# Attention and feed-forward block on 8 cores: the softmax normalisation of a group of heads moved behind the next group's first exponentials

## The reference

```python
qkv = encodings @ attn_w.T + attn_b
q, k, v = split(qkv per head)                      # heads of 64
scores = einsum('bhki,bhqi->bhkq', k, q) / sqrt(64)
scores = where(key <= query, scores, -10000.0)
probs = softmax(scores, over keys)
combined = einsum('bhkq,bhkl->bhql', probs, v)
x = x + combined @ out_w.T + out_b
...
s = layernorm(x) @ Win + bin_                      # 1024 -> 64
h = relu(s[..., None] * W1 + b1)                   # 64 x 16
g = einsum('btmh,mh->btm', h, W2) + b2
x = x + g @ Wout + bout
```

## Time and profile before

| what | value |
|---|---|
| three runs, median (lowest to highest) | 4349.49 us (4315.81 to 4365.05) |
| the profiled execution | 4315.81 us |
| its span on the slowest core (core 1) | 4313.9 us |
| spans of the 8 cores | 4290.3 to 4313.9 us |
| busy: TensorE, its weight loads, VectorE, ScalarE, GpSimd | 65%, 25%, 26%, 42%, 4% |
| mean granted clock of TensorE (1.0 is 2.4 GHz) | 0.760 |

### The profile page before, as it was taken

The page is one execution under the profiler, slowest core; times in us unless marked ns, Lnnn a source line. Parts: engine busy times, 40 slices in busy tenths (PEclk is TensorE's granted clock), DMA queues, the critical chain, the costliest instruction groups (busy, mean ns, idle before and its releaser), DMA issues.

```text
span 4313.9 us, 40195 instructions; the slowest of 8 cores (4290.3 to 4313.9 us)
## 1 busy us (share of the span) xinstructions
PE 2800.6 (65%) x12288; PEld 1074.8 (25%) x12288; DVE 1110.9 (26%) x2486; ACT 1804.1 (42%) x2945; POOL 167.3 (4%) x324
## 2 busy tenths in 40 slices
PE   0657576586656658677674766767667576765874
PEld 0223232232222223222231322223222132322321
DVE  3141321401324141230223223132132413214112
ACT  0324337166141624617523261643733234272481
POOL 0000000000000000000000000000000000000000
PEclk9768688698676868778776776878877677776886
DMA  6010000100101010010000001000000100000000
GB/s 198 11 38 19 23 30 15 42 7 15 40 20 40 15 35 15 16 40 10 20 30 30 30 20 40 10 20 30 15 25 25 35 25 25 30 15 30 10 10 25
DMA packets 38984, 122.02 MB, mean 28 GB/s; under 512 B 9658, under 2 KB 9786, under 8 KB 38780
## 3 DMA queue, kind: packets, MB, share of 16 engines
q0 software_dynamic: 21504, 67.13, 4.4%
q1 hardware_dynamic: 17020, 51.80, 4.1%
q10 hardware_dynamic: 256, 0.52, 0.0%
HBM read 85.34 MB, written 34.08 MB: 28 GB/s over the span
## 4 chain that ended last, share of the span: by engine, by line
PE 48%; ACT 15%; DVE 12%; issue 11%; DMA 11%; DVEq 0%; ACTq 0%; SPq 0%; POOLq 0%; POOL 0%
PE P L314 10%; PE P L389 10%; ACT s_probs L361 7%; DMA s_zz<-zscr 7%; PE P L291 6%; PE P L448 6%; PE P L352 5%; DVE s_xln L219 2%; DMA zscr<-s_zz 2%; ACT s_zz L407 2%; ACT s_zz L404 2%; DVE s_comb L425 2%; DVE s_probs L491 2%; PE P L543 2%; PE P L547 2%
## 5 line engine op out<-in xcount | busy, mean ns | idle before, releaser
L361 ACT ACTIVATE s_probs<-P 128x1024 bf16<-128x1024 f32 (+3 forms) x1280 | 1063.5, 895 | 376.9 <-PE P L356 305.7
L389 PE MATMUL P<-s_probs,s_vaug 128*65 128x512 bf16 (+3 forms) x2560 | 720.7, 399 | 173.4 <-DVE s_comb L425 94.8
L352 PE MATMUL P<-s_q,s_k 64*128 64x512 bf16 (+3 forms) x1280 | 464.8, 391 | 435.6 <-ACT s_probs L361 402.1
L369 DVE TENSOR_TENSOR s_probs<-s_probs,s_tril 128x256 bf16<-128x256 bf16 x512 | 145.8, 292 | 1403.8 <-ACT s_probs L361 1400.9
L448 PE MATMUL P<-s_ow,s_comb 128*128 128x512 bf16 x1024 | 357.9, 509 | 190.1 <-DVE s_comb L425 150.9
L356 PE MATMUL P<-s_q,s_k 64*128 64x512 bf16 (+3 forms) x1280 | 473.9, 398 | 0.0
L314 PE MATMUL P<-s_xlnT,s_wqk 128*128 128x512 bf16 x2048 | 448.8, 381 | 0.0
L389 PEld LDWEIGHTS P<-s_probs,s_vaug 128*65 128x65 bf16 x2560 | 247.9, 119 | 536.8 <-issue 441.1
L237 ACT ACTIVATE s_stats<-s_stats 128x1 f32<-128x1 f32 x128 | 37.7, 295 | 762.6 <-DVE s_stats L234 762.6
L480 PE MATMUL P<-s_id,s_xln 128*128 128x128 bf16 x512 | 107.9, 258 | 370.9 <-ACT s_probs L487 279.1
L425 DVE TENSOR_TENSOR s_comb<-P,s_zz 64x512 bf16<-64x512 f32 x256 | 174.9, 683 | 643.8 <-DMA s_zz<-zscr 639.5
(11 more groups left out here) (58 smaller groups left out, 2024.9 us busy)
## 6 DMA issues: line engine op xcount, KB each, us to landing
s_x<-x SPq DMA_DIRECT2D x64, 512.0 KB, 3.7
s_zz<-zscr POOLq DMA_DIRECT2D x256, 128.0 KB, 3.0
out<-s_x POOLq DMA_DIRECT2D x64, 512.0 KB, 2.9
s_x<-wqk_t SPq DMA_DIRECT2D x16, 512.0 KB, 7.6
s_x<-wv_t SPq DMA_DIRECT2D x8, 512.0 KB, 6.2
s_x<-ow_t SPq DMA_DIRECT2D x8, 512.0 KB, 7.2
zscr<-s_zz ACTq DMA_DIRECT2D x128, 4.0 KB
s_x<-bias_rows SPq DMA_DIRECT2D x1, 260.0 KB
```

The source lines that it names most:

```text
L352: s.op("pe", lambda E, c=hp, k=kt, c0=col0, S=SC: E.matmul(S[:, c0:512], s_k[0:64, c * T + k * 128: c * T + (k + 1) * 128], s_q[0:64, c * ...
L361: texp = s.op("act", lambda E, S=SC, pb=prb, c0=col0: E.activation(pb[:, :].rearrange("p (h c) -> p h c", h=2, c=512)[:, :, c0:512], S.rea ...
L369: dep_pv = s.op("dve", lambda E, pb=prb, c0=col0: E.tensor_tensor(pb[:, :].rearrange("p (h c) -> p h c", h=2, c=512)[:, :, c0:c0 + 128], p ...
L389: P=pv_banks[bank]: E.matmul(P[:, c0:512], s_vaug[:, ti * NH * 65 + hh2 * 65: ti * NH * 65 + hh2 * 65 + 65], pb[:, hi2 * 512 + c0: hi2 * 5 ...
```

## The change

The normalisation of a group is put into a function `norms`, whose arguments hold the group's pairs and its last value products, and is not called at the end of the group. It is called in the next group's loop, once the scores and exponentials of key tile 0 of both pairs have been issued and before those of key tile 1. For the last group of a stage it is called after the loop over u, where it stood before.

```diff
@@ attention
             comb_written = []
+            pending_norms = None
             for u in range(4):
...
                         newpend = (kt, col0, deps_pv, probs)
+                        if kt == 0 and pending_norms is not None:
+                            pending_norms()
+                            pending_norms = None
                     if pending is not None:
...
                     pending = newpend
-                for pi, hp in enumerate(pairs):
+
+                def norms(pairs=pairs, t_last_pv=t_last_pv):
+                  for pi, hp in enumerate(pairs):
                     t_lp = t_last_pv[pi]
...
                     st_["zz_read"][pi] = comb_written[-1]
+
+                pending_norms = norms
+            pending_norms()
             st_["P1_freed"] = comb_written[-1]
```

## The result

| | before | after |
|---|---|---|
| median of 12 runs each | 4341.80 us | 4408.16 us |
| ratio after to before (95% interval) | | 1.0204 (1.0163 to 1.0245) |
| the profiled execution | 4315.81 us | 4408.10 us |
| span of its slowest core | 4313.9 us | 4406.2 us |
| mean granted clock of that core | 0.760 | 0.756 |

The changed kernel is 2% slower. Between the two profiled executions lie 92.3 us.

What follows compares the result with a forecast made beforehand. No engine bounds the span; each group step ends with the chain Ln, Exp, write, broadcast, multiplication. 36 x 2.4 + 12 x 0.8 = 96 us gave 4412 on the profiled execution's scale, 4445 on the median's; range 4400 to 4505.

Steps and rivals of the forecast that it cites:

- The count and the place: Cost only at 48 steps between head groups: 36 long, 12 short (stages of 4 key tiles); stage ends unchanged.
- Ln 2.4 us later: On ScalarE at each group step, Ln starts behind two exponentials of key tile 0: 1021.65 instead of 1019.24.
- The chain behind Ln is only shifted: Write, broadcast and multiplication keep their distances after Ln, so each long step grows by 2.4 us.
- Short step +0.8: In 4-key-tile stages, masks of key tile 0 ahead of the multiplications get back 1.6 of 2.4 us.
- Sum 96 us, 4412 on the profiled execution's scale: All steps: 36 x 2.4 + 12 x 0.8 us, added to the profiled execution's 4315.8 us.
- The figure on the median's scale: The 96 us sum added to 4349.5 us, the median of three earlier runs: 4445 us.
- The clock is neutral: TensorE's granted clock in the group steps was taken to add or save nothing.
- clock rival: TensorE's clock returns later (4507 us; 0.14, shared with other growing waits) or stays high (4374 us; 0.05).
- 8 us without a product: Expected sign on TensorE in the group step: a wait of about 8 us, 1022 to 1030.
- The rule of the Trainium skill: Making a gap's dependencies start sooner helps; the change starts the multiplication's chain later, so the step gets longer.
- their end at 1028.47: In a long step before, four score exponentials ended 4.25 us before TensorE could offer new scores, so cost nothing.

Runs made afterwards that it cites:

- masks_first: Kernel before with only VectorE's four multiplications moved behind the masks of key tile 0; Ln, Exp and DMAs unmoved: ratio 0.9948.
- the series 0, 1, 2, 4: Kernels with that many of the new group's exponentials ahead of the normalisation, 0 being the kernel before: ratios 1, 1.012, 1.020 and 1.041.

## Why the prediction was right

The forecast was 4445 us, 2.2% more than the median; measured were 4408 (within the range of 4400 to 4505) and 2.04%. By its own steps:

- *The count and the place* (36 long and 12 short steps, nothing elsewhere): right. TensorE's three waits named above grew by 93.2 us, the change in the short stages alone gave 12 us, and by the traces the rest lies in the long steps.
- *Ln 2.4 us later*: measured 2.5 at the median. The two parts were 0.52 us from scores to exponential and 1.96 for the two exponentials (1033.86 to 1035.82), where 1.87 had been worked out.
- *The chain behind Ln is only shifted*: nearly. From Ln to the last multiplication's end it took 12.3 us over the steps in place of 12.5, so the long step grew by 2.38 though Ln came 2.5 later. The two places are the second write with its wait (2.8 us in place of 2.95 at the median up to the broadcast) and the way from Ln to the first multiplication (7.1 in place of 7.2); why these are shorter no run tells.
- *Short step +0.8*: +0.73, and the 1.6 us that it gets back from VectorE's order were shown alone by masks_first.
- *Sum 96 us, 4412 on the profiled execution's scale*: 92.3 and 4408.1. The figure on the median's scale came out 37 us too high: 4 us by the sum, 8 by the median before (4341.8 over 12 runs in place of 4349.5 over three), and the rest since the changed kernel's median stands at its profiled execution and that of the kernel before 26 us above it. What was off is the choice of scale and not the mechanism.
- *The clock is neutral*: right. It was at 0.50 of full where the products resume, in both kernels, and came back after 4.9 us in both. Neither clock rival took place. TensorE waited 7.4 us at the median for the first value product of a long step, where 8 us without a product had been forecast.
- *The rule of the Trainium skill* (Perfetto Trace Analysis, Optimization Strategy), to make what a gap waits for start sooner, gave the right sign here (Ln 2.5 us later, 2% slower). Followed, and not gone against as by the change, it gave two gains: by freeing the banks before the chain (0.950) and by getting the second write out earlier (0.974).

Each point above except the slightly shorter chain rests on a run. That the exponentials were free where they stood is shown by the series 0, 1, 2, 4: each costs its full time ahead of Ln, so it can't have cost anything behind it. I had argued it from their end at 1028.47 in the earlier trace rows. 4408 lies near the lower end of the range, since 4445 was built on a median of three runs that stood 34 us above the fastest; the ratio and the steps are the better test.

## What to carry to other kernels

Before moving work ahead of a wait, ask which chain ends the wait and whether the moved work was already hidden inside it: here two exponentials of 1 us were free behind the start of a 12 us chain through DRAM, and cost their full time ahead of it. Start the long chain first and fill its latency; and better, take the shared buffer (here the PSUM bank) off the chain by copying it out, which together with issuing both Ln first was worth 5%. And when a wait changes its name between two profiles, add up all waits of that engine in the stage before reading one of them: one row here rose by 377 us where the kernel lost 92.

## What the hardware showed that I had not expected

In this kernel a small DMA took longer when a broadcast had been issued just before it. From the issue of the 4 KB write to the start of the broadcast that waits for it, it took 1.8 us with the DMA engines otherwise empty. It took 3.2 us in the step shown, and 2.95 at the median of the 64 groups, when the issue of two broadcasts of 128 KB each had begun 0.95 us earlier; issued 0.3 us ahead of these broadcasts it took 1.8 us again. The DMA packets in the traces show where the time went. The 4 KB left 0.74 us after the issue of a first write. That of the second write in the step shown left 1.79 us after its issue, at 1026.14, while the broadcasts' packets ran from 1024.84 to 1026.38. With both Ln first it left after 0.74 us again, in all 64 groups. The other order was worth 2.6% of the kernel. The releaser given in the profile for this wait (the multiplication on VectorE) was one that the program doesn't wait for at that point.
